# Routed expert visits with the tokens as the stationary operand, gate and up in one 256 column result, and a transpose ahead of the down step

## What is computed

```
routing = softmax(x @ gate_w.T); topw, sel = top_k(routing, 2)       # 16 experts, 2 for each token
hmid = silu(x @ w1[e].T) * (x @ w3[e].T)                              # gate and up, 128 wide, input 512 wide
moe_out = sum over the chosen e of combine[e] * (hmid @ w2[e].T)      # down, output 512 wide
shared = silu(x @ ws_gate.T) * (x @ ws_up.T) @ ws_down.T              # 512 wide, every token
out = x + moe_out + sigmoid(x @ shared_gate_w.T) * shared
```

## The kernel before

| position | engine | what |
|---|---|---|
| V-4 | PE | `row_transposes`: 4 transposes of the tile (128x512) from `hm` into bank 1 or 0 |
| V-2 | ACT | `rows`: copy of them to xT (L702), releases `rows_ready` |
| V, V+1 | PE | `gate_up`: 4 matmuls for gate, then 4 for up (L1445), weights held still, 128 token columns moved |
| V+3 | ACT | `tanh_g` (L708) |
| V+4, V+5 | DVE | `expert_gate` (L932), `expert_up` (L939): the gated product, feature rows x token columns |
| V+7 | PE | `down` (L1469): one matmul with the product held still and 512 columns moved |
| V+9 | ACT | `y_rows` (L719): copy of the result, releases `y_ready` |

## Time and profile before

### The profile page before, as it was taken

One profiled execution on the slowest core, in us unless ns is written; L12 is line 12 of the kernel. 1 busy time (PEld: TensorE's weight loads), 2 busy tenths in 40 slices (PEclk: granted clock), 3 DMA queues, 4 the chain that ended last, 5 costly groups with the idle time before them and its releaser, 6 DMA issues.

```text
span 2011.6 us, 19064 instructions
## 1 busy us (share of the span) xinstructions
PE 1493.4 (74%) x5208; PEld 831.6 (41%) x5208; DVE 1595.8 (79%) x2477; ACT 728.3 (36%) x1232; POOL 1010.7 (50%) x611
## 2 busy tenths in 40 slices
PE   6846567994578898895578898885587988647873
PEld 2212122442345564332344564332254654336662
DVE  2699999678998998688998999588998999674111
ACT  3434343243323554234323554133323554021221
POOL 0159999101658887301558888301458988301001
PEclk9977878997689999997689999997788999867997
DMA  2252000321224664321324664411413764402785
GB/s 94 87 194 87 0 1 25 130 98 63 108 96 137 209 220 162 127 106 32 136 79 141 205 220 153 160 66 57 152 59 125 220 214 153 168 0 86 254 285 170
DMA packets 99016, 255.25 MB, mean 127 GB/s; under 512 B 11488, under 2 KB 11616, under 8 KB 93792
## 3 DMA queue, kind: packets, MB, share of 16 engines
q1 hardware_dynamic: 91680, 233.08, 34.7%
q0 software_dynamic: 5120, 16.78, 2.5%
q10 hardware_dynamic: 2112, 4.19, 0.5%
HBM read 211.02 MB, written 42.99 MB: 126 GB/s over the span
## 4 chain that ended last, share of the span: by engine, by line
DVE 30%; PE 26%; POOL 19%; issue 17%; DMA 3%; ACT 3%; SPq 1%; DVEq 0%; POOLq 0%; ACTq 0%
POOL work L535 10%; DVE bank L908 7%; DVE du L890 5%; PE bank L1445 4%; PE bank L1548 4%; PE bank L1350 3%; DMA ew_up<-in_exp_w 3%; PE bank L1391 2%; POOL work L543 2%; DVE u L863 2%; PE bank L1379 2%; POOL pairs L543 1%; PE bank L1397 1%; DVE pairs L916 1%; POOL work L546 1%
## 5 line engine op out<-in xcount | busy, mean ns | idle before, releaser
L535 POOL TENSOR_TENSOR work<-du,BB 128x1024 f32<-128x1024 f32 x256 | 604.3, 2367 | 4.7 <-DVE bank L908 4.2
L683 ACT ACTIVATE bank<-delta,A_sb 128x512 f32<-128x512 f32 x512 | 351.0, 690 | 640.2 <-DVE pairs L916 397.8
L908 DVE TENSOR_TENSOR_SCAN bank<-bank,work 128x512 f32<-128x512 f32 x448 | 543.1, 1220 | 46.9 <-POOL work L535 46.9
L1445 PEld LDWEIGHTS bank<-xT,ew_up 128*128 128x128 f32 x1472 | 195.7, 198 | 102.5 <-issue 78.6
L1445 PE MATMUL bank<-xT,ew_up 128*128 128x128 f32 x1472 | 204.2, 284 | 33.9 <-DMA ew_up<-in_exp_w 19.9
L1360 PE MATMUL bank<-xT,wst 128*128 128x512 f32 x256 | 132.6, 672 | 82.5 <-ACT zg L640 82.5
L916 DVE TENSOR_TENSOR pairs<-bank,CB 128x512 f32<-128x512 f32 x256 | 172.4, 674 | 10.3 <-PE bank L1391 9.0
L502 POOL TENSOR_TENSOR delta<-delta,pairs 128x512 f32<-128x512 f32 x32 | 51.5, 1610 | 234.4 <-DVE pairs L891 234.4
L1469 PE MATMUL bank<-ew_dn,etm 128*128 128x512 f32 x184 | 105.2, 655 | 36.5 <-ACT xT L719 36.5
L916 DVE TENSOR_TENSOR work<-bank,CB 128x512 f32<-128x512 f32 x192 | 128.8, 671 | 0.0
L1445 PE MATMUL bank<-x3T,ew_up 128*128 128x256 f32 x512 | 124.6, 400 | 0.7 <-DMA ew_up<-in_exp_w 0.6
(11 more groups left out here) (185 smaller groups left out, 2573.0 us busy)
## 6 DMA issues: line engine op xcount, KB each, us to landing
ew_up<-in_exp_w SPq DMA_DIRECT2D x124, 512.0 KB, 3.7
ew_dn<-in_exp_w SPq DMA_DIRECT2D x124, 256.0 KB, 4.3
hm<-xs_dram SPq DMA_DIRECT2D x92, 256.0 KB, 4.5
ys_dram<-xT SPq DMA_DIRECT2D x92, 256.0 KB, 4.5
wst<-in_w_in SPq DMA_DIRECT2D x64, 256.0 KB, 2.6
BB<-bc_dram SPq DMA_DIRECT2D x16, 1024.0 KB, 4.9
CB<-bc_dram SPq DMA_DIRECT2D x16, 1024.0 KB, 7.0
wst<-in_out_w SPq DMA_DIRECT2D x32, 256.0 KB, 2.7
```

Source lines behind the costliest of these rows:

```text
L535: nc.gpsimd.tensor_tensor(dBu[:, k % CHUNK_SLOTS, :, :], du[:, j % 2:j % 2 + 1, :].broadcast_to([P, 2, T]), BB[:, n0:n0 + 2, :], ALU.mult) ...
L683: nc.scalar.activation(R[q % RING][:, :], delta[:, j, :], ACT.Exp, scale=A_sb[:, j, n:n + 1]).then_inc(S["da_ready"], 1)
L908: V.tensor_tensor_scan(prod[c % (2 * PAIR_SLOTS)] if on_pool(c) else R[q % RING][:, :], R[q % RING][:, :], dBu[:, c // 2 % CHUNK_SLOTS, c ...
L1445: ins = mm(gu_bank(v)[:, part * n:(part + 1) * n], ew_up[:, q % UP_RING, part * D + k * P:part * D + (k + 1) * P], rhs, start=(k == 0), st ...
```

## The change

Only routed visits are changed. The transposed tokens become the stationary operand and the weights move: 4 matmuls of 256 columns give token rows x (gate, up) in one result, and so the weights of gate and up lie interleaved in memory, for the shared visits too, whose matmuls are otherwise as before. The product then has token rows, so a PE transpose (`turn`) and an ACT copy (`turned`) turn it before `down`, which reads the second half of eT's slot. The turned block uses bank 0, as the row transposes do, and each of the two waits for the other's copy. With V for the position of the visit the order is now: row transposes V-3 (was V-4), gate and up in one piece at V, `tanh_g` V+2, `expert_gate` V+3, `expert_up` V+4 (each one earlier), `turn` V+5, `turned` V+6, `down` V+8 (was V+7), `y_rows` V+10 (was V+9). SP's order and DVE's wait at L931 are not touched.

```
-ROWS_BEFORE = 4
+ROWS_BEFORE = 3
+TURN_BEHIND = 5
+TURN_COPY_BEHIND = 6
+ROUTED_DOWN_BEHIND = 8
-Y_COPY_BEHIND = 9
+Y_COPY_BEHIND = 10
...
+        def rows_ahead(r):
+            return len([i for i in range(ROUTED)
+                        if VISIT_AT[SHARED + i] - ROWS_BEFORE < VISIT_AT[SHARED + r] + TURN_BEHIND])
+        def turns_ahead(r):
+            return len([i for i in range(ROUTED)
+                        if VISIT_AT[SHARED + i] + TURN_BEHIND <= VISIT_AT[SHARED + r] - ROWS_BEFORE])
...
+                def turned(r):
+                    v = SHARED + r
+                    sc.wait_ge(S["turn_ps"], ROUTED * (b - 1) + r + 1)
+                    nc.scalar.copy(eT[:, v % 2, P:2 * P], turn_bank[:, 0:P]).then_inc(S["turn_ready"], 1)
...
-                            if VISIT_AT[v] + T1_BEHIND == p:
+                            if VISIT_AT[v] + T1_BEHIND - (v >= SHARED) == p:
                                 expert_gate(v)
...
+                    if r >= 2 and turns_ahead(r) > 0:
+                        pe.wait_ge(S["turn_ready"], ROUTED * (b - 1) + turns_ahead(r))
...
+                def routed_gate_up(v):
+                    q, n = VISITS * (b - 1) + v, ROUTED * (b - 1) + v - SHARED
+                    pe.wait_ge(up_in[q % UP_RING], 16 * (q // UP_RING + 1))
+                    wait(pe, "t2_done", q if v == SHARED else q - 1)
+                    pe.wait_ge(S["rows_ready"], n + 1)
+                    for k in range(KD):
+                        ins = mm(gu_bank(v)[:, 0:2 * P], xsT[n % 2][:, k, :],
+                                 ew_up[:, q % UP_RING, 2 * k * P:2 * (k + 1) * P], start=(k == 0), stop=(k == KD - 1))
+                    ins.then_inc(S["gu_done"], 1)
+                def turn(v):
+                    q, r = VISITS * (b - 1) + v, v - SHARED
+                    pe.wait_ge(S["t2_done"], q + 1)
+                    pe.wait_ge(S["rows_ready"], ROUTED * (b - 1) + rows_ahead(r))
+                    if r > 0:
+                        pe.wait_ge(S["turn_ready"], ROUTED * (b - 1) + r)
+                    else:
+                        pe.wait_ge(S["shared_done"], TT * b)
+                    nc.tensor.transpose(turn_bank[:, 0:P], eT[:, v % 2, 0:P], ident[:]).then_inc(S["turn_ps"], 1)
                 def down(v):
-                    pe.wait_ge(S["t2_done"], q + 1)
+                    if v < SHARED:
+                        pe.wait_ge(S["t2_done"], q + 1)
+                    else:
+                        pe.wait_ge(S["turn_ready"], ROUTED * (b - 1) + v - SHARED + 1)
...
-                        mm(down_ps[1][:, :], eT[:, v % 2, 0:P], ew_dn[:, q % DOWN_RING, :],
+                        mm(down_ps[1][:, :], eT[:, v % 2, P:2 * P], ew_dn[:, q % DOWN_RING, :],
                            start=True, stop=True).then_inc(S["down_done"], 1)
```

More of the change, by code:

```diff
@@ L234, in rows_bank @@
             return bank[1] if r < 2 else bank[0]
+        turn_bank = bank[0]
+        def rows_ahead(r):
[4 more added lines that the diff above has]
+                        if VISIT_AT[SHARED + i] + TURN_BEHIND <= VISIT_AT[SHARED + r] - ROWS_BEFORE])
         def width(v):
@@ L249, in build @@
             "du_ready dbu_ready da_ready scan_done prod_done pair_ready pool_prod nsum_done y_done "
-            "rows_ps rows_ready gu_done eth_ready t1_done t2_done down_done shared_done y_ready "
+            "rows_ps rows_ready gu_done eth_ready t1_done t2_done turn_ps turn_ready down_done shared_done y_ready "
             "mix_done out_done zeros xs_zeroed scattered ys_back route_ready rank_ps rank_copied route_done "
@@ L734, in scan_stage @@
                         for v in range(VISITS):
-                            if VISIT_AT[v] + TANH_BEHIND == p:
+                            if VISIT_AT[v] + TANH_BEHIND - (v >= SHARED) == p:
                                 tanh_g(v)
@@ L739, in scan_stage @@
                                 rows(r)
+                            if VISIT_AT[SHARED + r] + TURN_COPY_BEHIND == p:
+                                turned(r)
                             if VISIT_AT[SHARED + r] + Y_COPY_BEHIND == p:
@@ L982, in scan_stage @@
                         for v in range(VISITS):
-                            if VISIT_AT[v] + T1_BEHIND == p:
+                            if VISIT_AT[v] + T1_BEHIND - (v >= SHARED) == p:
                                 expert_gate(v)
-                            if VISIT_AT[v] + T2_BEHIND == p:
+                            if VISIT_AT[v] + T2_BEHIND - (v >= SHARED) == p:
                                 expert_up(v)
@@ L1436, in gate_up @@
                         pe.wait_ge(up_in[q % UP_RING], 16 * (q // UP_RING + 1))
-                        wait(pe, "t2_done", q if v == SHARED else q - 1)
+                        wait(pe, "t2_done", q - 1)
                         if v == RANK_VISIT:
                             pe.wait_ge(S["rank_copied"], b)
-                        if v >= SHARED:
-                            pe.wait_ge(S["rows_ready"], ROUTED * (b - 1) + v - SHARED + 1)
                     for k in range(KD):
-                        rhs = (x3T[:, k, v // NSH * TH:(v // NSH + 1) * TH] if v < SHARED else
-                               xsT[(ROUTED * (b - 1) + v - SHARED) % 2][:, k, :])
                         ins = mm(gu_bank(v)[:, part * n:(part + 1) * n],
-                                 ew_up[:, q % UP_RING, part * D + k * P:part * D + (k + 1) * P], rhs,
+                                 ew_up[:, q % UP_RING, (2 * k + part) * P:(2 * k + part + 1) * P],
+                                 x3T[:, k, v // NSH * TH:(v // NSH + 1) * TH],
                                  start=(k == 0), stop=(k == KD - 1))
@@ L1480, in scan_stage @@
                         for v in range(VISITS):
-                            if VISIT_AT[v] + DOWN_BEHIND == p:
+                            if VISIT_AT[v] + (DOWN_BEHIND if v < SHARED else ROUTED_DOWN_BEHIND) == p:
                                 down(v)
-                            if p in (VISIT_AT[v], VISIT_AT[v] + 1):
+                            if v >= SHARED and VISIT_AT[v] + TURN_BEHIND == p:
+                                turn(v)
+                            if v < SHARED and p in (VISIT_AT[v], VISIT_AT[v] + 1):
                                 gate_up(v, p - VISIT_AT[v])
+                            if v >= SHARED and VISIT_AT[v] == p:
+                                routed_gate_up(v)
                             if v >= SHARED and VISIT_AT[v] - ROWS_BEFORE == p:
@@ L1543, in mixer_out @@
                     wait(pe, "rows_ready", ROUTED * m)
+                    wait(pe, "turn_ready", ROUTED * m)
                     wait(pe, "t2_done", VISITS * m)
@@ L1652 @@
     w2 = np.concatenate([a["L0_ffn_w2"], a["L0_ffn_ws_down"].reshape(D, NSH, P).transpose(1, 0, 2)])
-    up = [np.concatenate([blocks(w, P)[0] for w in ws])[None].reshape(NE + NSH, P, D) for ws in (w1, w3)]
+    up = np.stack([np.concatenate([blocks(w, P)[0] for w in ws]).reshape(NE + NSH, P, KD, P) for ws in (w1, w3)], axis=3)
     arrays = {
@@ L1668 @@
         "gate_w": cols(np.concatenate([a["L0_ffn_gate_w"], a["L0_ffn_shared_gate_w"]])),
-        "exp_w": np.concatenate([up[0], up[1], np.ascontiguousarray(w2.transpose(0, 2, 1))], axis=2),
+        "exp_w": np.concatenate([up.reshape(NE + NSH, P, 2 * D), np.ascontiguousarray(w2.transpose(0, 2, 1))], axis=2),
     }
```

## The result

The changed kernel takes 2038.3 us (median of 4, 2031.3 to 2044.6), the kernel before, on the same chip, 2008.0 (2005.9 to 2014.2). The ratio is 1.0144, 95% interval 1.0109 to 1.0178: slower by about 29 us. The direction was forecast; the size was not. The forecast had +10.8 us, and 2038.3 lies above the range's upper end of 2034. The profiled execution took 2037.84 us, 23.9 more than that of before.

The account below looks back on a forecast made before the run. DVE was taken to set the pace beside the scans, with TensorE close behind, and transfers in the last stage. Terms 6.0 + 3.3 + 0 + 1.5 = +10.8 us gave 2017.7 us on the median; range 1998 to 2034.

Parts of the forecast that it names:

- The streams: TensorE, routed visits: 8 records of 256 columns take 1.73 us; with the extra transpose +0.06 us a visit, hidden, counted nothing.
- ACT: ScalarE's added copy `turned`: 0.28 us each, 6.4 us in a stage where ACT waits far longer for DVE; counted nothing.
- The tighter order beside the scan: Scan stages: `expert_gate` waits for `down`, now one position ahead; two stalls of about 1 us a stage, +6.0 us in all.
- the margin of 1 us: Beside the scans: `down` ends near 1171.75, ahead of `expert_gate` before the scan at 1172.69; gone when TensorE runs at half clock.
- the last rival: DVE waits at most visits: TensorE's order uses up the margin; +34.5 us, 2046 with the ends, 2029 at half; chance 0.12.
- The end of the visits beside the scan: End of each scan stage: last result copied one position later, gather starts 1.1 us later; +3.3 us for three stages.
- The last stage: Loop over `ew_up` transfers and matmul groups: 0.93 us leaves the group, +1.35 comes before the next issue; taken as 0.
- later requests meet a shorter queue: Last stage: `ew_up` requests issued later may land sooner, so the net +0.42 us a pair need not stay.
- faster through the last stage: Rival: shorter group counts, the two issues ahead don't; 320 GB/s reached, -8.7 us; 2003.0, or 1994.6 without DVE stalls; chance 0.20.
- The very end: After the last group: first of the last `down`s follows the group, +1.0, small copies and turns +0.5; together +1.5 us.

Follow-up runs that it names:

- e6: Kernel before, with only TensorE's order changed: down of visit r-2 put behind up of visit r at V+1, no position moved; 1992.38 us, ratio 0.993.
- e9: Changed kernel with the result copy one position earlier, at V+9, and nothing else; 2015.55 us, ratio 1.0057.
- e4: Kernel before, matmuls unchanged, with only the positions of the routed visits' tail shifted as in the change; 2011.94 us, ratio 1.0025.
- e2: Changed kernel, but expert_gate waits for the turn of visit r-2 instead of its down, and the turned copy waits for that down; 2009.63 us, ratio 1.0052.
- e8: Changed kernel timed and profiled once more, unaltered, to see how profiles scatter; 2035.32 us, ratio 1.0134.
- e1: Changed kernel with SP issuing ew_up ahead of the tile load and the store; 2021.72 us, ratio 1.0089.
- e5: Changed kernel with the edits of e1 and e2 together, and the result copy at V+9; 1992.01 us, ratio 0.9931.
- e11: Changed kernel with SP's gate and up loads for the next batch held until all gathers have landed; 2024.09 us, ratio 1.0077.
- e12: Kernel of e6 with SP's gate and up loads for the next batch held until all gathers have landed; 1978.09 us, ratio 0.9866.

## Why the prediction had the direction and not the size

- *The streams*: right. 8 records of 256 columns take 1.73 to 2.0 us at the full clock, TensorE's sum rose by 5.6 us, and e6 has the gain of the last stage without the new form. The new form without the turn was not tried.
- *ACT*: the small copy takes 0.26 us (taken: 0.28). But "I count nothing" is a step that failed, by what stands behind it on TensorE: the row transposes wait for this copy, 14 times, 17.8 us between 500 and 1790, 19 times where the result's copy is out of the way (e9). By e4 some 7 to 12 us of A come with the turned product and what hangs on it, all of which the sum had at nothing. How much of that is this one wait no run separates.
- *The tighter order beside the scan*: right in place and mechanism (e2 takes it away), mis-sized. 6.0 us were forecast, 13.1 and 10.5 measured, 14 and 13 waits instead of 6. For the shift alone, which is what was worked out, e4 has 7.6 us in 8 waits, close to the 6.0. The value was taken "near the small end"; the margin of 1 us was worked out at one place with the result's copy alone ahead of `down`. The order on TensorE (turn, 256 column group, row transposes, each with a wait on ScalarE) belongs in it, which is what the last rival named; its +17 (0.5 us at half of 69 visits) and the forecast's +6 lie on either side of the 13.1.
- *The end of the visits beside the scan*: right in mechanism, 3.3 forecast, 6.4 measured, 4.2 where no store took longer than 2 us to land.
- *The last stage*: the other step that failed, and this one in kind. "Since bytes bind and they are unchanged, I take 0": +6.3 measured, beyond the bound of +4.2 (C in e8: +4.1). The two halves were seen and are real: the shorter group (e4 and e6: -10.9 and -7.9 in C) and the two issues and transposes ahead of `ew_up` (e1: -14.8 when undone, some 6 of it by the clock). Neither is absorbed by the transfers: a DMA share of 0.90 at 288 GB/s was not the limit, since e1 and e5 hold 0.97 at 324 and 328, and the kernel before 0.96 at 316 over 14 us. That "later requests meet a shorter queue" did not show either, with landings of 4.9 us against 4.7. The clock of this stage had no term. The rival "faster through the last stage" had the point on the bytes right, and wrong that the two issues do not count. The Trainium skill, "DMA: Bandwidth & Descriptors", section Specifications, has about 358 GB/s as HBM's limit for a core. In the last stages of all these runs windows of 10 us stay at 346 GB/s or less. But the measurement decides, and it is no limit here: the kernel before moves 378 GB/s from 140 to 160 us, where SP stores `x3T` to `xs_dram`.
- *The very end*: +1.5 forecast, +0.2 measured.

With the measured sizes, 13.1 + 6.4 + 6.3 + 0.2 = 26.0, against 24.2 between the spans. So the direction was forecast for reasons that hold, and the size failed by the turned product beside the scans and by the order in SP's queue, each taken at 0.

Open: what delays `down` in each of the 14 visits, copy of the result or turned copy, since moving one lets the other hold it; and how far A would fall in the changed kernel if the turn had a bank of its own, which was not tried.

## What to carry to other kernels

A loop between a transfer and a group of matmuls is priced by everything from the group's last instruction to the next issue, and a DMA share of 0.90 does not make that free. Look for a shorter stretch with a higher share before you call it the limit, and put the transfer that the loop waits for ahead of the others in an in-order queue, and check what each request ahead of it now waits for. When an operation moves toward its user, ask which buffer really has to be free: the turn had already released what `expert_gate` overwrites. And before a form of matmul is changed for its stream time, try the order alone: here the order alone had 14 us (e6, 0.9930), and the changed form with three repairs came no lower (e5, 0.9931).

## What the runs showed of the hardware

The eighth indirect gather of a run of eight on POOL comes later after the seventh than the others after theirs (0.16 to 0.31 us). With SP's two loads of 1 MB held back it waits 3.5 to 4.1 us (e11, e12), and in the last stages, where there are no such loads, 3.2 to 3.4. In the 36 scan stages of the other twelve profiles it goes by the time from the start of the seventh gather to the first of the two loads: 1.7 us or more, a wait of 3.1 to 3.8 us (10 stages); 1.5 or 1.6 us, 4.3 (2 stages); 0.8 us or less, down to a load that comes first, 6.2 to 8.3 (23 of 24 stages, 4.9 in the other). Why the eighth waits at all is open. Between the profiles of e6 and e12 the gathers' three stretches shrink by 8.2 us and the stretches from the last gather to the next stage by 3.2, of the 17.4 us between their spans (13 as timed).
